# A three-layer graph attention network on one core: the first item's rows turned in the accumulator banks, and a new order of the prologue

## The chip, the core and the metric

The kernel runs on one core of a Trainium2 chip. Its engines work side by side, each through its own list of instructions in order: TensorE (PE, matmuls and their weight loads), VectorE (DVE), ScalarE (ACT), GpSimd (POOL) and SyncE (SP), whose queue issues all DMA transfers here. Engines wait for each other only through semaphores. The metric is the time of one execution on the device in microseconds.

## What is computed

64 graphs of 128 nodes with 256 features each. The input is normalised and cut at zero, three layers of attention over the adjacency and of a two-matrix feed-forward part follow, and the input is added at the end:

```
h = jnp.maximum(_layernorm(x, axis=-1), 0.0)
for l in range(3):
    si = x @ attn_w[l, :d];  sj = x @ attn_w[l, d:]
    scores = si[:, :, None] + sj[:, None, :] + attn_b[l]
    scores = jnp.where(scores >= 0, scores, 0.2 * scores)
    attn = jax.nn.softmax(jnp.where(mask, scores, -jnp.inf), axis=-1)
    agg = jnp.einsum('bij,bjd->bid', attn, x)
    h = layernorm(x + agg, g1[l], beta1[l])
    ff = jax.nn.gelu(h @ W1[l] + b1[l], approximate=False) @ W2[l] + b2[l]
    x = layernorm(h + ff, g2[l], beta2[l])
```

(the loop starts from x = h; the result is the kernel's input plus the last x).

## The kernel before

An **item** is four graphs in one layer: 16 groups of four graphs times three layers, 48 items, in batches of four groups. The work is a pipeline over items. In slot s the feed-forward part of item s runs on TensorE, while the other engines prepare items s + 1 to s + 4. The slots are one written list for each engine, the same for all s. Ahead of the first slot every engine has a **prologue**, written out by hand for items i0 to i3; its order is what the change is about.

One item goes through these steps. Names are the functions of the code.

- `input_moments`, `input_shift` (DVE), `make_rstd` (POOL), `first_x` (ACT): the first normalisation, only in layer 0. `penalty` (DVE) turns the adjacency into a mask.
- `j_dots`, `i_dots` (DVE): the two dot products of every node. The sj values go to DRAM and come back as rows for all partitions (`send_sj`, `load_sj` on SP, tile sj_bc); only item 0 takes them through TensorE (`sj_rows`).
- `masked`, `minus_max` (DVE), `leaky`, `exps` (ACT): scores, row maximum, exponentials in sc.
- The exponentials are turned. Items 0 and 1 (q < BY_PE) do it on TensorE (`e_turn`, into util) and ScalarE copies them out (`et_out`). Later items use `turn_e` (DVE) and DMA (`send_e`, `move_e`).
- `aggregate` (PE) into the banks mix, then `attend`, `moments1`, `norm1` (DVE, with `make_rstd` on POOL between the last two). `h_gamma` and `h_beta` (POOL) make the residual's copy.
- The rows are turned for the matmuls, in two sets of four 128 by 128 blocks. Items 0 and 1 do it on TensorE (`z1_turn`, into util), later ones on VectorE and DMA. ScalarE scales and rounds them (`h_out`, `h_high`, tile ht_hi), VectorE makes what is left over (`h_low`, tile ht_lo).
- The feed-forward part works in eight **chunks** of hidden rows. `ffn1` is six matmuls into one of three banks hbank, ScalarE computes gelu and the rounded copy (`gelu_high`, tile hid_hi), VectorE the low half (`low`, tile hid_lo), `ffn2` is twelve matmuls into the two accumulator banks acc. `ffn1` of a chunk waits until `low` of the chunk three before is done, `ffn2` of a chunk until its own `low` is done.
- `residual`, `moments2`, `shift2` (DVE), `norm2` (ACT), `x_gamma`, `x_beta` (POOL) close the item.

Weights come in 12 halves, four for each layer: `load_weights` (SP), rounded by `round_weights` (ACT), the rest by `split_weights` (DVE). The first eight loads lie in the prologue, and halves 4 to 7 wait for a staging tile that an earlier half leaves.

PSUM has eight banks: three hbank, two acc, two mix and one util. Util is used by all turns on TensorE, and each of them waits until the reader of the one before is done:

```
            def wait_util_read():
                wait(pe, eto_n, read["e"])
                wait(pe, htlo_n, read["z"])
                wait(pe, mask_n, read["s"])
```

So the second set of item 0's rows can't be written before ht_lo of the first set is made, and the first set not before the exponentials of item 1 have been copied out. The acc banks are empty until the first `ffn2`.

Of the kernel before, what the change touches and what calls it, by code (L numbers as in the profile page):

```python
# [33 lines left out]
P = 128  # L34
# [22 lines left out]
def build(nc, x, adj, attn_w, attn_b, W1, b1, W2, b2, g1, beta1, g2, beta2, out):  # L57
# [19 lines left out]
    with ExitStack() as ctx:  # L77
# [232 lines left out]
        def _(sp):  # L310
# [153 lines left out]
            load_xraw(item(2))  # L464
            load_adj(item(2))
            load_weights(4)
            send_sj(i1)
            load_xraw(i3)
            load_sj(i1)
            send_sj(i2)  # L470
            load_weights(5)
            load_adj(i3)
            load_sj(i2)
            load_weights(6)
            send_e(i2)
            send_sj(i3)
            move_e(i2)
            load_sj(i3)
            load_ln2_rows()
            load_attn_rows(False)  # L480
            load_weights(7)
            for s in range(1, ITEMS + 3):
# [10 lines left out]
        def _(pool):  # L493
# [119 lines left out]
            make_rstd("0", i0.g)  # L613
            make_rstd("0", i1.g)
            make_rstd("0", i2.g)
            bias_rows()
            make_rstd("1", i0.q)
            h_gamma(i0, 0)
            h_gamma(i0, 1)
            h_beta(i0, 0)  # L620
            make_rstd("0", i3.g)
            make_rstd("1", i1.q)
            h_beta(i0, 1)
            h_gamma(i1, 0)
            make_rstd("1", i2.q)
            h_gamma(i1, 1)
            h_gamma(i2, 0)
            h_beta(i1, 0)
            for s in range(1, ITEMS + 3):
# [5 lines left out]
        def _(dve):  # L635
# [289 lines left out]
            masked(i0)  # L925
            split_weights(0)
            minus_max(i0)
            j_dots(i1)
            split_weights(1)
            split_weights(2)  # L930
            input_moments(i2)
            i_dots(i1)
            attend(i0, 0)
            input_shift(i2)
            masked(i1)
# [3 lines left out]
            j_dots(i2)  # L939
            penalty(i2)  # L940
            norm1(i0)
            input_moments(i3)
            h_low(i0, 0)
            attend(i1, 0)
            masked(i2)
            h_low(i0, 1)
            attend(i1, 1)
            i_dots(i2)
            moments1(i1)
            split_weights(3)  # L950
            minus_max(i2)
            penalty(i3)
            low(i0, 0)
            input_shift(i3)
            norm1(i1)
            turn_e(i2)
            low(i0, 1)
            split_weights(4)
            j_dots(i3)
            low(i0, 2)  # L960
            low(i0, 3)
            split_weights(5)
            low(i0, 4)
            low(i0, 5)
            h_low(i1, 0)
            i_dots(i3)
            low(i0, 6)
            attend(i2, 0)
            masked(i3)
            attend(i2, 1)  # L970
            h_low(i1, 1)
            moments1(i2)
            minus_max(i3)
            low(i0, 7)
            low(i1, 0)
            norm1(i2)
            residual(i0, 0)
            residual(i0, 1)
            for s in range(1, ITEMS + 3):
# [5 lines left out]
        def _(act):  # L985
# [20 lines left out]
            def h_out(i, m):  # L1006
                if i.q < BY_PE:
                    act.wait_ge(zt_n, KD * i.q + m + 1)
                    if i.q == 0 and m == 0:
                        act.wait_ge(vec_ready, 1)  # L1010
                    act.activation(util[:], util[:], ACT.Identity, bias=beta1c(i.l, m),
                                   scale=g1c(i.l, m)).then_inc(ht_n, 1)
# [81 lines left out]
            first_x(i0)  # L1094
            round_weights(0)
            round_weights(1)
            round_weights(2)
            first_x(i1)
            leaky(i0)
            round_weights(3)  # L1100
            exps(i0)
            et_out(i0)
            first_x(i2)
            leaky(i1)
            exps(i1)
            et_out(i1)
            h_high(i0, 0)
            round_weights(4)
            h_high(i0, 1)
            round_weights(5)  # L1110
            gelu_high(i0, 0)
            leaky(i2)
            exps(i2)
            gelu_high(i0, 1)
            first_x(i3)
            gelu_high(i0, 2)
            gelu_high(i0, 3)
            gelu_high(i0, 4)
            h_high(i1, 0)
            gelu_high(i0, 5)  # L1120
            gelu_high(i0, 6)
            h_high(i1, 1)
            gelu_high(i0, 7)
            leaky(i3)
            gelu_high(i1, 0)
            gelu_high(i1, 1)
            round_weights(6)
            exps(i3)
# [5 lines left out]
        def _(pe):  # L1134
# [114 lines left out]
            e_turn(i1)  # L1249
            z1_turn(i0, 0)  # L1250
            aggregate(i1, 0)
            aggregate(i1, 1)
            z1_turn(i0, 1)
            ffn1(i0, 0)
            ffn1(i0, 1)
            ffn1(i0, 2)
            ffn1(i0, 3)
            ffn2(i0, 0)
            z1_turn(i1, 0)
            ffn2(i0, 1)  # L1260
            ffn1(i0, 4)
            ffn1(i0, 5)
            ffn1(i0, 6)
            ffn2(i0, 2)
            ffn2(i0, 3)
            ffn1(i0, 7)
            aggregate(i2, 0)
            aggregate(i2, 1)
            z1_turn(i1, 1)
            ffn2(i0, 4)  # L1270
            ffn2(i0, 5)
            ffn1(i1, 0)
            ffn1(i1, 1)
            ffn2(i0, 6)
            ffn2(i0, 7)
            ffn1(i1, 2)
# [24 lines left out]
```

## Time and profile before

| | us |
|---|---|
| median of 3 runs (1233.28 to 1233.67) | 1233.32 |
| the profiled execution | 1233.53 |
| its span, first to last instruction | 1231.7 |
| TensorE busy | 1190.9 (97%) |
| VectorE busy | 1058.8 (86%) |
| ScalarE busy | 988.7 (80%) |
| GpSimd busy | 677.0 (55%) |

The page gives busy time for each engine over the whole span. Since the kernel is one pipeline with a start and an end, such a share doesn't say where an engine stood still. For that there are the list of waits (who waited for whom, for how long), the windows (busy time of each engine in a stretch, with TensorE's granted clock, 1.00 for full and 0.50 for half), the timeline (instructions in order) and the chain that ended last.

### The profile page before, as it was taken

How to read it: one execution, taken by the hardware profiler on the slowest of the kernel's cores; microseconds unless marked ns; L12 is line 12 of the kernel's file. 1: busy time of each engine (PE TensorE's matmuls, PEld its weight loads, DVE VectorE, ACT ScalarE, POOL GpSimd, SP SyncE). 2: the span in 40 equal slices, each digit the busy share in tenths (PEclk: the TensorE clock that was granted, in tenths of full speed). 3: DMA queues.
4: the chain of work that ended last, by engine and by line, in shares of the span. 5: the costliest groups of instructions: out<-in, count | busy, mean ns of one | idle time of the engine just before them, and what ended most of it. 6: DMA issues, size and time to landing. Idle time of an engine off the chain costs nothing.

```text
span 1231.7 us, 23195 instructions
## 1 busy us (share of the span) xinstructions
PE 1190.9 (97%) x7325; PEld 1086.1 (88%) x7325; DVE 1058.8 (86%) x3483; ACT 988.7 (80%) x1944; POOL 677.0 (55%) x648
## 2 busy tenths in 40 slices
PE   2799999999999999999999999999999999999997
PEld 1698999999899999999999999999999999999996
DVE  7889888899998888889998888889999888888754
ACT  5777888789888887888888778878888788788853
POOL 2326544556675455546765555455657554645474
PEclk9799999999999999999999999999999999999999
DMA  7243233235432322244344222233454222222322
GB/s 235 62 144 87 78 117 87 73 95 154 147 112 81 102 76 61 85 115 123 116 129 128 87 61 86 88 86 87 126 156 134 83 86 86 69 61 91 116 70 69
DMA packets 142744, 124.73 MB, mean 101 GB/s; under 512 B 16632, under 2 KB 123164, under 8 KB 142620
## 3 DMA queue, kind: packets, MB, share of 16 engines
q1 hardware_dynamic: 142620, 123.23, 33.6%
q8 instruction: 58, 0.95, 0.3%
q14 instruction: 66, 0.54, 0.2%
HBM read 78.53 MB, written 44.66 MB: 100 GB/s over the span
## 4 chain that ended last, share of the span: by engine, by line
PE 92%; DVE 4%; ACT 1%; POOL 1%; issue 1%; DMA 0%; SPq 0%; DVEq 0%; POOLq 0%
PE acc L1164 43%; PE hbank L1149 41%; PE mix L1181 7%; DVE junk L768 0%; DVE xs L836 0%; DVE hid_lo L667 0%; DMA adji<-in_adj_dram 0%; DVE st L843 0%; ACT xs L1061 0%; POOL rstd L511 0%; DVE xs L849 0%; DVE junk L777 0%; DVE sc L804 0%; DVE st L655 0%; POOL hb L538 0%
## 5 line engine op out<-in xcount | busy, mean ns | idle before, releaser
L1164 PE MATMUL acc<-w2hi,hid_hi 128*128 128x256 f32 x1536 | 443.5, 289 | 1.3 <-DVE hid_lo L667 1.3
L1164 PE MATMUL acc<-w2hi,hid_lo 128*128 128x256 f32 x1536 | 434.9, 283 | 0.0
L1164 PE MATMUL acc<-w2lo,hid_hi 128*128 128x256 f32 x1536 | 434.7, 283 | 0.0
L994 ACT ACTIVATE hbank<-hbank,vec 128x512 f32<-128x512 f32 x384 | 254.4, 662 | 139.6 <-PE hbank L1149 133.8
L1149 PE MATMUL hbank<-ht_hi,w1hi 128*128 128x512 f32 x768 | 303.2, 395 | 4.7 <-DVE hid_lo L667 3.7
L1164 PEld LDWEIGHTS acc<-w2hi,hid_hi 128*128 128x128 f32 x1536 | 294.6, 192 | 12.8 <-DVE hid_lo L667 2.4
L1164 PEld LDWEIGHTS acc<-w2lo,hid_hi 128*128 128x128 f32 x1536 | 293.9, 191 | 10.4
L1149 PE MATMUL hbank<-ht_lo,w1hi 128*128 128x512 f32 x768 | 302.4, 394 | 0.0
L1149 PE MATMUL hbank<-ht_hi,w1lo 128*128 128x512 f32 x768 | 299.4, 390 | 0.0
L667 DVE TENSOR_TENSOR hid_lo<-hbank,hid_hi 128x512 fp32r<-128x512 f32 x384 | 258.9, 675 | 41.5 <-ACT hid_hi L1000 41.1
L1164 PEld LDWEIGHTS acc<-w2hi,hid_lo 128*128 128x128 f32 x1536 | 293.8, 191 | 0.0
L1000 ACT CAST hid_hi<-hbank 128x512 fp32r<-128x512 f32 x384 | 225.8, 588 | 12.9 <-PE acc L1164 0.8
L531 POOL TENSOR_TENSOR hb<-xs,ln_rows 128x512 f32<-128x512 f32 x96 | 123.5, 1303 | 151.6 <-DVE xs L681 111.6
L550 POOL TENSOR_TENSOR xs<-xs,ln_rows 128x512 f32<-128x512 f32 x64 | 82.9, 1295 | 179.2 <-DVE dots L777 179.0
L1149 PEld LDWEIGHTS hbank<-ht_hi,w1lo 128*128 128x128 f32 x768 | 144.7, 188 | 32.0
L1149 PEld LDWEIGHTS hbank<-ht_hi,w1hi 128*128 128x128 f32 x768 | 145.5, 189 | 29.4 <-DVE hid_lo L667 4.3
L1149 PEld LDWEIGHTS hbank<-ht_lo,w1hi 128*128 128x128 f32 x768 | 145.6, 190 | 21.0
L509 POOL TENSOR_SCALAR ve<-mv 128x4 f32<-128x4 f32 x111 | 30.4, 274 | 175.8 <-DVE mv L646 175.7
L538 POOL TENSOR_TENSOR hb<-hb,ln_rows 128x512 f32<-128x512 f32 x96 | 124.9, 1301 | 0.0
L511 POOL TENSOR_TENSOR rstd<-ve,halfs 128x4 f32<-128x4 f32 x111 | 118.4, 1067 | 9.3
L836 DVE SCALAR_TENSOR_TENSOR xs<-mix,rden,xs 128x256 f32<-128x256 f32 x192 | 83.7, 478 | 42.4 <-PE mix L1181 41.6
L768 DVE CUSTOM_DVE_ANT_0 junk<-xs,attn_rows 128x256 bf16<-128x256 f32 x192 | 76.6, 455 | 35.5 <-ACT xs L1030 35.1
(91 smaller groups left out, 1777.7 us busy)
## 6 DMA issues: line engine op xcount, KB each, us to landing
z_dram<-tz SPq DMA_DIRECT2D x46, 512.0 KB, 2.6
zt<-z_dram SPq DMA_DIRECT2D x184, 128.0 KB, 3.0
sj_bc<-sj_dram SPq DMA_DIRECT2D x47, 256.0 KB, 3.6
e_dram<-te SPq DMA_DIRECT2D x46, 256.0 KB, 2.0
ET<-e_dram SPq DMA_DIRECT2D x184, 64.0 KB, 2.1
out_dram<-xout SPq DMA_DIRECT2D x32, 256.0 KB, 4.0
xraw<-in_x_dram SPq DMA_DIRECT2D x15, 512.0 KB, 5.1
xres<-in_x_dram SPq DMA_DIRECT2D x15, 512.0 KB, 4.3
```

Source lines behind the costliest of these rows:

```text
L511: pool.tensor_tensor(rstd[n][:], ve[n][:], halfs[:], ALU.pow).then_inc(rstd_n[n], 1)
L531: pool.tensor_tensor(hb[:, i.q % 2, gs], x_of(i)[:, gs], rows_of(ln1_rows[:, 0], i.l), ALU.mult).then_inc(hgam_n, 1)
L538: pool.tensor_tensor(t, t, rows_of(ln1_rows[:, 1], i.l), ALU.add).then_inc(hb_n, 1)
L550: pool.tensor_tensor(t, t, rows_of(ln2_rows[:, 0], i.l), ALU.mult).then_inc(gam_n, 1)
L667: dve.tensor_tensor(hid_lo[:, k % HID], hbank[k % HB][:], hid_hi[:, k % HID].bitcast(F32), ALU.subtract).then_inc(lo_n, 1)
L768: last = dve.tensor_tensor_reduce(junk[:, g], x_of(i)[:, g], attn_rows[:, i.l, 1], 1.0, 0.0, ALU.mult, ALU.add, dots[:, 1, g:g + 1])
L836: dve.scalar_tensor_tensor(out=x_of(i)[:, g], in0=mix_of(i, h)[:, g % HG], scalar=rden[:, g:g + 1], in1=x_of(i)[:, g], op0=ALU.mult, op1=A ...
L994: act.activation(hbank[k % HB][:], hbank[k % HB][:], ACT.Gelu, bias=b1c(i.l, c)).then_inc(gelu_n, 1)
L1000: act.copy(hid_hi[:, k % HID], hbank[k % HB][:]).then_inc(hi_n, 1)
L1149: mm = pe.matmul(hbank[k % HB][:], w[:, i.l, m, at_c], v[:, i.q % 2, m], start=m == 0 and n == 0, stop=m == KD - 1 and n == 2)
L1164: mm = pe.matmul(to, v[:, k % HID, of_g], w[:, i.l, c], start=c == 0 and n == 0 and g % HG == 0, stop=c == C - 1 and n == 2, skip_group_ch ...
L1181: mm = pe.matmul(mix_of(i, h)[:, g % HG], turned, x_of(i)[:, g], start=g % HG == 0, stop=True, skip_group_check=True)
```

## The change

Two things change, both ahead of the first slot.

First, `z1_turn` of item 0 writes its two sets into acc[0] and acc[1] instead of util, without waiting for util's readers; `h_out`, `h_high` and `h_low` of item 0 read them there. Item 1 goes on using util.

```
+        def turned_in(q, m):
+            if q == 0:
+                return acc[m][:].rearrange("p g d -> p (g d)")
+            return util[:]
...
             def z1_turn(i, m):
-                wait_util_read()
+                if i.q > 0:
+                    wait_util_read()
+                t = turned_in(i.q, m)
                 read["z"] += 1
                 for g in range(GG):
                     pe.wait_ge(z1_n, GG * i.q + g + 1)
-                    mm = pe.transpose(util[:, g * P:(g + 1) * P], x_of(i)[:, g, m * P:(m + 1) * P], ident[:])
+                    mm = pe.transpose(t[:, g * P:(g + 1) * P], x_of(i)[:, g, m * P:(m + 1) * P], ident[:])
                 mm.then_inc(zt_n, 1)
...
-                dve.tensor_tensor(ht_lo[:, i.q % 2, m], util[:], ht_hi[:, i.q % 2, m].bitcast(F32),
+                dve.tensor_tensor(ht_lo[:, i.q % 2, m], turned_in(i.q, m), ht_hi[:, i.q % 2, m].bitcast(F32),
...
-                act.copy(ht_hi[:, i.q % 2, m], util[:]).then_inc(hthi_n, 1)
+                act.copy(ht_hi[:, i.q % 2, m], turned_in(i.q, m)).then_inc(hthi_n, 1)
```

Second, the prologue's lists of all five engines are written in another order, with the same calls in each. The slots and the end are as they were. On SP the send of item 1's sj values now goes ahead of weight half 4, item 3's adjacency and weight half 5 go ahead of the send for item 2, and weight half 7 ahead of the load for item 3:

```
             load_xraw(item(2))
             load_adj(item(2))
+            send_sj(i1)
             load_weights(4)
-            send_sj(i1)
             load_xraw(i3)
+            load_adj(i3)
             load_sj(i1)
+            load_weights(5)
             send_sj(i2)
-            load_weights(5)
-            load_adj(i3)
             load_sj(i2)
```

On GpSimd `bias_rows` goes ahead of item 2's `make_rstd`, the `h_gamma` steps of item 1 ahead of the second `h_beta` of item 0.

TensorE, from the turn of item 1's exponentials to the first matmul of `ffn1`. L1206 and L1213 are `z1_turn`, L1181 and L1186 `aggregate` of item 1. Before:

```order
L1214 MATMUL util<-ident,sc 128x128 x4
L1206 MATMUL util<-ident,xs 128x128 x4
L1181 MATMUL mix0<-xs,ET 128x256 x2
L1181 MATMUL mix1<-xs,ET 128x256 x2
L1206 MATMUL util<-ident,xs 128x128 x4
L1149 MATMUL hbank0<-ht_hi,w1hi 128x512
```

and in the changed kernel:

```order
L1221 MATMUL util<-ident,sc 128x128 x4
L1213 MATMUL acc0<-ident,xs 128x128 x4
L1213 MATMUL acc1<-ident,xs 128x128 x4
L1186 MATMUL mix0<-xs,ET 128x256 x2
L1186 MATMUL mix1<-xs,ET 128x256 x2
L1154 MATMUL hbank0<-ht_hi,w1hi 128x512
```

Both sets of item 0 now stand ahead of item 1's aggregation. Further on, the fifth chunk of `ffn1` stands ahead of the first `ffn2`, and item 1's first turn moves from behind the first chunk of `ffn2` to behind its fourth.

VectorE, around the first low halves of hidden rows (tile hid_lo; te is the turn of item 2's exponentials, the TENSOR_SCALAR on xs is `norm1` of item 1, BN_STATS st1 its `moments1`). Before:

```order
L843 BN_STATS st1<-xs 128x6 x4
L644 MEMSET spare 128x1
L646 BN_AGGR mv1<-st1 128x2 x4
L639 TENSOR_TENSOR w2lo<-xres,w2hi 128x1024
L812 ISA below,spare<-msj,dots 128x4
L812 ISA spare 128x1
L788 SCALAR_TENSOR_TENSOR pen<-adji,diag 128x512
L792 TENSOR_SCALAR pen<-pen 128x512
L667 TENSOR_TENSOR hid_lo<-hbank0,hid_hi 128x512
L661 SCALAR_TENSOR_TENSOR nmr0<-mv0,rstd0 128x4
L849 TENSOR_SCALAR xs<-xs,mv1,rstd1 128x256 x4
L820 STREAM_TRANSPOSE te<-sc 128x4x4x32
```

and in the changed kernel:

```order
L672 TENSOR_TENSOR hid_lo<-hbank1,hid_hi 128x512
L644 TENSOR_TENSOR w2lo<-xres,w2hi 128x1024
L817 ISA below,spare<-msj,dots 128x4
L817 ISA spare 128x1
L841 SCALAR_TENSOR_TENSOR xs<-mix1,rden,xs 128x256 x2
L672 TENSOR_TENSOR hid_lo<-hbank2,hid_hi 128x512
L644 TENSOR_TENSOR w1lo<-xout,w1hi 128x1024
L666 SCALAR_TENSOR_TENSOR nmr0<-mv0,rstd0 128x4
L672 TENSOR_TENSOR hid_lo<-hbank0,hid_hi 128x512
L848 BN_STATS st1<-xs 128x6 x4
L649 MEMSET spare 128x1
L651 BN_AGGR mv1<-st1 128x2 x4
```

Four low halves (the first stands a few rows further up) are now ahead of the moments of item 1; before, the first stood behind them.

ScalarE, from the first gelu on (sc,den is `exps` of item 2, the ACTIVATE on sc,dots its `leaky`). Before:

```order
L994 ACT_TABLE_LOAD
L994 ACTIVATE hbank0<-hbank0,vec 128x512
L1000 CAST hid_hi<-hbank0 128x512
L1037 ACTIVATE sc<-sc,dots 128x128 x4
L1042 ACTIVATE negm<-below 128x4
L1047 ACT_TABLE_LOAD
L1047 ACTIVATE sc,den<-sc,negm 128x128 x4
L994 ACT_TABLE_LOAD
L994 ACTIVATE hbank1<-hbank1,vec 128x512
```

and in the changed kernel:

```order
L999 ACTIVATE hbank0<-hbank0,vec 128x512
L1005 CAST hid_hi<-hbank0 128x512
L999 ACTIVATE hbank1<-hbank1,vec 128x512
L1005 CAST hid_hi<-hbank1 128x512
L999 ACTIVATE hbank2<-hbank2,vec 128x512
L1005 CAST hid_hi<-hbank2 128x512
L1042 ACTIVATE sc<-sc,dots 128x128 x4
L999 ACTIVATE hbank0<-hbank0,vec 128x512
L1005 CAST hid_hi<-hbank0 128x512
L1047 ACTIVATE negm<-below 128x4
L1052 ACT_TABLE_LOAD
L1052 ACTIVATE sc,den<-sc,negm 128x128 x4
```

The exponentials of item 2, with a table load on each side, stand behind four gelus instead of one. The roundings of weight halves 4 and 5 move from between the high halves of item 0 to the front and behind item 1's exponentials.

## Rows read from the trace of the kernel before

**Rows 1.** The page, part 1: busy time, share of the span, instructions.

```profile
PE 1190.9 (97%) x7325; PEld 1086.1 (88%) x7325; DVE 1058.8 (86%) x3483; ACT 988.7 (80%) x1944; POOL 677.0 (55%) x648
```

**Rows 2.** TensorE's waits (total, times, longest) to 110 and later; timeline at 94.42.

```profile
PE hbank L1149 <- DVE hid_lo L667: 3.2, 1, 3.2
PE acc L1164 <- DVE hid_lo L667: 1.3, 1, 1.3
...
PE hbank L1149 <- DVE hid_lo L667: 0.5, 1, 0.5
...
94.42 0.38 PE L1164 MATMUL acc<-w2hi,hid_hi 128*128 128x256 f32 x1 [1.25 <-DVE hid_lo L667]
```

**Rows 3.** Windows: length, busy time of each engine, granted clock, DMA share, GB/s.

```profile
28.97:77.03 48.06, 40.02 (x199) 33.92 (x200) 41.90 (x138) 35.94 (x75) 14.45 (x15) 0.82 0.29 88
...
76.99:94.42 17.43, 16.18 (x100) 14.69 (x98) 16.46 (x50) 14.18 (x29) 7.97 (x8) 1.00 0.44 130
```

**Rows 4.** Timeline of VectorE: start, us, instruction, idle before.

```profile
28.97 1.41 DVE L843 BATCH_NORM_STATS2 st<-xs 128x6 f32<-128x256 f32 x4
...
30.71 0.39 DVE L768 CUSTOM_DVE_ANT_0 junk<-xs,attn_rows 128x256 bf16<-128x256 f32 x1
...
32.07 0.68 DVE L788 SCALAR_TENSOR_TENSOR pen<-tz,diag 128x512 bf16<-128x512 int32 x1
...
33.00 2.32 DVE L849 TENSOR_SCALAR xs<-xs,mv,rstd 128x256 f32<-128x256 f32 x4
35.24 1.39 DVE L655 BATCH_NORM_STATS2 st<-xraw 128x6 f32<-128x256 f32 x4
...
41.55 0.69 DVE L855 TENSOR_TENSOR ht_lo<-util,ht_hi 128x512 fp32r<-128x512 f32 x1 [1.02 <-ACT ht_hi L1023]
...
44.56 1.40 DVE L843 BATCH_NORM_STATS2 st<-xs 128x6 f32<-128x256 f32 x4
```

**Rows 5.** Timeline of GpSimd: the root of item 0's variance.

```profile
31.28 1.07 POOL L511 TENSOR_TENSOR rstd<-ve,halfs 128x4 f32<-128x4 f32 x1
```

**Rows 6.** The chain that ended last, pieces on TensorE: start, us, what.

```profile
35.85 3.41 PE mix L1181 x8
39.26 0.87 PE util L1206 x4
...
49.16 2.92 PE hbank L1149 x6
52.08 2.56 PE acc L1164 x12
...
70.16 2.75 PE hbank L1149 x12
72.91 2.89 PE acc L1164 x24
```

**Rows 7.** Timeline of ScalarE at the first gelu.

```profile
42.48 1.28 ACT L994 ACT_TABLE_LOAD   x1
43.78 0.66 ACT L994 ACTIVATE hbank<-hbank,vec 128x512 f32<-128x512 f32 x1
44.47 0.59 ACT L1000 CAST hid_hi<-hbank 128x512 fp32r<-128x512 f32 x1
```

**Rows 8.** Timeline of VectorE: the normalisations of items 1 and 2.

```profile
49.11 3.29 DVE L849 TENSOR_SCALAR xs<-xs,mv,rstd 128x256 f32<-128x256 f32 x4
...
73.51 1.60 DVE L849 TENSOR_SCALAR xs<-xs,mv,rstd 128x256 f32<-128x256 f32 x4
```

**Rows 9.** Windows of half a microsecond; the third number from the end is the clock.

```profile
41.00:41.50 0.50, 0.33 (x1) 0.00 (x0) 0.00 (x0) 0.50 (x2) 0.00 (x0) 0.88 0.00 0
47.50:48.00 0.50, 0.00 (x0) 0.00 (x0) 0.50 (x3) 0.38 (x2) 0.42 (x2) 0.95 0.00 0
```

**Rows 10.** Tiles sj_bc and xout (weights) up to 90: transfers, issue to landing.

```profile
DMA to landing us min/median/max: 3.6/3.7/5.5
...
DMA to landing us min/median/max: 3.6/5.0/7.1
```

More of the change, by code:

```diff
@@ L465, in _ @@
             load_adj(item(2))
+            send_sj(i1)
             load_weights(4)
-            send_sj(i1)
             load_xraw(i3)
+            load_adj(i3)
             load_sj(i1)
+            load_weights(5)
             send_sj(i2)
-            load_weights(5)
-            load_adj(i3)
             load_sj(i2)
+            send_e(i2)
             load_weights(6)
-            send_e(i2)
+            move_e(i2)
             send_sj(i3)
-            move_e(i2)
+            load_weights(7)
             load_sj(i3)
@@ L943, in _ @@
             h_low(i0, 0)
+            penalty(i2)
+            h_low(i0, 1)
             attend(i1, 0)
+            i_dots(i2)
+            low(i0, 0)
             masked(i2)
[L946 to L949, printed above, removed]
+            low(i0, 1)
             split_weights(3)
             minus_max(i2)
-            penalty(i3)
[L953 to L967, printed above, removed]
+            attend(i1, 1)
+            low(i0, 2)
+            split_weights(4)
+            input_shift(i3)
+            low(i0, 3)
+            moments1(i1)
+            turn_e(i2)
+            split_weights(5)
+            norm1(i1)
+            low(i0, 4)
+            j_dots(i3)
+            low(i0, 5)
+            i_dots(i3)
+            h_low(i1, 0)
+            low(i0, 6)
+            penalty(i3)
             attend(i2, 0)
+            low(i0, 7)
+            attend(i2, 1)
             masked(i3)
-            attend(i2, 1)
             h_low(i1, 1)
             moments1(i2)
+            residual(i0, 0)
             minus_max(i3)
-            low(i0, 7)
+            residual(i0, 1)
             low(i1, 0)
             norm1(i2)
-            residual(i0, 0)
-            residual(i0, 1)
             for s in range(1, ITEMS + 3):
@@ L1010, in h_out @@
                         act.wait_ge(vec_ready, 1)
-                    act.activation(util[:], util[:], ACT.Identity, bias=beta1c(i.l, m),
-                                   scale=g1c(i.l, m)).then_inc(ht_n, 1)
+                    t = turned_in(i.q, m)
+                    act.activation(t, t, ACT.Identity, bias=beta1c(i.l, m), scale=g1c(i.l, m)).then_inc(ht_n, 1)
                 else:
@@ L1095, in _ @@
             round_weights(0)
+            first_x(i1)
             round_weights(1)
-            round_weights(2)
-            first_x(i1)
             leaky(i0)
-            round_weights(3)
             exps(i0)
             et_out(i0)
+            round_weights(2)
+            round_weights(3)
             first_x(i2)
             leaky(i1)
+            round_weights(4)
             exps(i1)
+            round_weights(5)
             et_out(i1)
             h_high(i0, 0)
-            round_weights(4)
             h_high(i0, 1)
-            round_weights(5)
             gelu_high(i0, 0)
+            gelu_high(i0, 1)
+            gelu_high(i0, 2)
             leaky(i2)
+            gelu_high(i0, 3)
             exps(i2)
-            gelu_high(i0, 1)
+            gelu_high(i0, 4)
             first_x(i3)
-            gelu_high(i0, 2)
-            gelu_high(i0, 3)
-            gelu_high(i0, 4)
+            gelu_high(i0, 5)
             h_high(i1, 0)
-            gelu_high(i0, 5)
             gelu_high(i0, 6)
+            gelu_high(i0, 7)
+            round_weights(6)
             h_high(i1, 1)
-            gelu_high(i0, 7)
             leaky(i3)
@@ L1257, in _ @@
             ffn1(i0, 3)
+            ffn1(i0, 4)
             ffn2(i0, 0)
-            z1_turn(i1, 0)
             ffn2(i0, 1)
-            ffn1(i0, 4)
+            ffn2(i0, 2)
             ffn1(i0, 5)
             ffn1(i0, 6)
-            ffn2(i0, 2)
             ffn2(i0, 3)
+            z1_turn(i1, 0)
             ffn1(i0, 7)
+            ffn2(i0, 4)
+            ffn2(i0, 5)
             aggregate(i2, 0)
@@ L1269, in _ @@
             z1_turn(i1, 1)
-            ffn2(i0, 4)
-            ffn2(i0, 5)
+            ffn2(i0, 6)
+            ffn2(i0, 7)
             ffn1(i1, 0)
             ffn1(i1, 1)
-            ffn2(i0, 6)
-            ffn2(i0, 7)
             ffn1(i1, 2)
```

24 lines of the change are left out of this document (11 added, 13 removed).

## The prediction

> **What bounds the kernel now.** Start with the page: TensorE is busy for 1190.9 us of a span of 1231.7 [rows 1]. The list of who waits for whom shows how little of its idle time lies late: after 110 us it waits once, for 0.5 us, and the two last waits before that, 3.2 and 1.3 us, both for VectorE's low halves, lie in the first 95 us [rows 2]. Behind 95 us the program is TensorE's own work, which the change doesn't touch. What the change can move is the moment from which TensorE runs through, 94.42, when the 1.3 us wait ends [rows 2]. The windows say who sets it: from 28.97 to 77.03 TensorE has 40.02 us of work, part of it at half clock, and VectorE 41.90 in 48.06; from 76.99 to 94.42 TensorE has 16.18 in 17.43, with full clock [rows 3]. So at the last wait TensorE is ahead and VectorE, which works through a fixed order, is late. The question is how much sooner VectorE gets through its prologue, and then whether TensorE can follow.
>
> **Fixed marks.** All positions are microseconds of the profiled execution; i0 to i3 are items 0 to 3. VectorE's list ahead of the moments of i0 (28.97) holds the same operations in both kernels, and so does its list from there to the transpose of i2 that starts at 77.03; only the order differs. Up to 28.97 I find no gain and no loss: weight halves 1 and 2 are split behind i2's moments now, but ScalarE's exponentials of i0, which release the first aggregation, begin as before, and the aggregation is the later input.
>
> **Up to the first matmul of ffn1.** The moments of i0 run from 28.97 to 30.71, the dots of i2 to 32.07. Before, the penalty of i2 stood next (0.93) and the normalisation started at 33.00 [rows 4]. Now it stands there at once, but GpSimd's reciprocal root ends at 31.28 + 1.07 = 32.35 [rows 5], so VectorE waits 0.3, and the four instructions (2.24) end at 34.65 instead of 35.24: 0.6 sooner. TensorE turns the rows of i0 into the two accumulator banks, eight transposes in a row. Four took 0.87 [rows 6], so the first bank is complete at 35.3 and the second at 36.1; before, the second set shared util, stood behind the aggregation of i1, and was complete at 40.1. The price: the aggregation of i1 (3.41 for eight matmuls at half clock [rows 6]) starts at 36.1 instead of 35.85 and ends at 39.5. ScalarE and VectorE work on both banks under it, so the two low halves are done at 37.4 and 38.9. The first matmul of ffn1 starts at 39.5, and nothing interrupts the chunk.
>
> **VectorE's first real wait.** From 28.97 its work ahead of the first low half of hidden rows is moments twice 1.74, dots of i2 1.36, normalisation 2.24, penalty 0.93, a low half 0.6, the other low half with the attention update and the second dots 3.01 (41.55 to 44.56) and a reciprocal 0.2 [rows 4]: 11.8. With 0.3 for the root and 0.35 for the first high half it is free at 41.4. Six matmuls of ffn1 from 39.5, the first at 0.43 and the rest at 0.229 (2.75 for twelve [rows 6]), end at 41.4 to 41.7. Gelu and rounding start 0.69 apart and the rounding takes 0.59 [rows 7]: low half 0 starts at 42.7, after a wait of 1.3. The table load of 1.28 [rows 7] lies in ScalarE's empty time before 39.5 and costs nothing; without that cover it would cost its 1.28.
>
> **VectorE from there.** Its work in the whole stretch is 41.90 [rows 3]. Two items change length. The normalisation of i1 took 3.29 while GpSimd worked beside it on two steps; that of i2 took 1.60 and that of i0 2.32 [rows 4, 8]. In the new order GpSimd's beta step of i0 stands behind, so I take 2.3 for i1 (1.0 less) and 2.0 for i2, since a gamma step falls beside it (0.4 more). From 42.7 there remain 41.9 - 11.8 - 0.6 = 29.5, so the transpose of i2 starts at 72.2 if nothing is late. What each step needs, worked out on ScalarE with 1.18 per gelu and rounding: three of them end at 45.3, the leaky step of i2 at 46.5, gelu 3 at 47.7, then 0.2, a table load of 1.28 and exponentials of 1.6, done at 50.8; VectorE wants them at 51.5. A second table load and gelu 4 end at 53.3 (wanted at 56.0), the first inputs of i3 at 55.3 (56.6), gelu 5 at 56.5 (58.0). The last matmul of ffn2 for i0 ends at 66.1 (68.2), gelu 0 of i1 at 68.9 (69.6). All are covered, the tightest by 0.7. The copies of the score rows are less sure (rival 1), for which I add 0.2. Then 77.03 becomes 72.4: **4.6 us sooner**. The same from the waits: before, 48.06 - 41.90 = 6.2 us [rows 3]; now 0.3 + 0.35 + 1.3 + 0.2 = 2.1, and 0.6 less work: 4.7.
>
> **TensorE's side.** Chunks 0 to 2 of ffn1 run from 39.5, chunks 3 and 4 need low halves 0 and 1, done at 43.3 and 45.2: no gap, so the 3.2 us wait goes, and with it the half clock behind it, at which twelve matmuls of ffn2 took 2.56 against 1.45 [rows 6]. From 39.5: 11 chunks of ffn1 at 1.37, 8 of ffn2 at 1.45, 2.3 for the aggregation and the turns, 0.6 for the slow first matmuls and 1.3 of waiting near 56 for the normalisation of i1 and low half 4 give 70.4 for the prologue's last matmul, instead of 76.99: 6.6 sooner. VectorE grants only 4.6, so 2 us come back as new waits in the first slot, on low halves 1, 2 and 5 of i1 (0.8, 0.6 and about 1.6, against the one of 1.3). The lesser gain counts. In that slot nothing is reordered, and what VectorE waits for there, GpSimd's root and ScalarE's second normalisation, hangs on VectorE's own moments and moves with it. I take off 0.1 for small starts: **4.5**. The profiled execution took 1233.53 for its span of 1231.7; less 4.5 is 1229.0, and the median of the runs lies 0.2 below that execution: 1228.8.
>
> **The clock.** The granted clock is back at full by 41.5 (0.88 in the half microsecond before), after work without a break since 35.4, and falls just before 48 (0.95) [rows 9], two microseconds after TensorE went idle at 46.0, 3.2 ahead of 49.16 [rows 2, 6]. In the new order work is unbroken from 34.8, so the rise could come 0.6 sooner or at the same 41.1; I take the middle. If it came at 38, VectorE's 1.3 us wait would vanish. The 1.3 us wait before 94.42 did not cost the clock [rows 2, 3]; a wait of 1.6 lies between the cases. The Trainium skill, page "TensorE: Matmul & The Clock Gate", section "HAM oscillation — how this bites in real kernels", tells of a kernel whose TensorE fell back to the low clock in every wait between bursts. [...]
>
> **Rivals.** (1) Late row copies. VectorE's masks of i1 and i3 need the broadcast copy of sj, which landed 3.6 to 5.5 us after its issue [rows 10]. For i1 it is wanted at 26.8; the send now goes ahead of weight half 4, which helps, but i3's adjacency is queued ahead of the copy, which hurts. For i3 weight half 7 is queued just ahead; sent at 58.0 and two microseconds on its way, the copy lands at 63.6 to 65.5 and is wanted at 64.7. Each late microsecond is one of VectorE's. Late by 1.0 and 0.8, the gain is 2.9 and the time 1230.4. (2) The clock falls in the wait before low half 5, which may last 1.5 to 2.0. Half clock for some 5.5 us of work costs 2.7: gain 1.8, time 1231.5. (3) Early clock: gain 5.8, time 1227.5. (4) Slower. ScalarE's rounding of weight half 5 now stands ahead of the copy of i1's exponentials, and holds ScalarE and the aggregation of i1. Its load is issued behind the split of half 1, near 24; it is wanted at 32.1, with slack to 34. From there each microsecond costs one, so from a landing at 41 the kernel is slower by over 0.2%: 1237 with one at 42. Against it: the prologue's weight loads landed in 3.6 to 7.1 [rows 10], and it needs 17. (5) The waits only change place: something else in the first slot, such as GpSimd's order, keeps 94.42 within 1 us: 1232.5. Against it: GpSimd has little to do there.
>
> **How the numbers follow.** Forecast 0.52; late copies 0.14; clock 0.12; early clock 0.10; nothing reaches the end 0.08; slower 0.04. The range takes in the early clock, the forecast, the copies and the drop: 1227.0 to 1231.8. A measurement of this kernel tells about 0.2%, 2.5 us, from no change, so faster means below 1230.8: forecast, early clock, most of the late copies and a little of the rest, 0.77; same 0.19; slower 0.04.
>
> **What would show it.** Right: eight transposes into acc at 34 to 36, no wait of VectorE over 0.5 us between 43 and 72, its transpose of i2 at 72 to 73, TensorE at full clock from about 41, and waits on low halves of some 3 us in the first slot. Wrong: half clock after 85, a wait on sj_bc, a wait on weight half 5 near 32; and the whole reasoning, if 4.6 us at the transpose are not 4.6 us at the end.

## The result and the profile after

The changed kernel takes 1235.64 us (median of 20 runs, 1234.85 to 1238.47), the kernel before 1233.48 beside it (20 runs, 1232.87 to 1235.1). The ratio is 1.0018, 95% interval 1.0012 to 1.0024. By the bound of the prediction, 0.2%, that is no change; the interval says that it is a loss, of 2.2 us. The forecast was a gain of 4.5, with 1231.8 as the slowest time of its range. It was wrong.

The profiled execution took 1236.37, its span is 1234.6. The page, part 1, beside [rows 1]:

```profile
PE 1190.2 (96%) x7325; PEld 1083.7 (88%) x7325; DVE 1064.1 (86%) x3483; ACT 988.3 (80%) x1944; POOL 676.9 (55%) x648
```

TensorE has the same work. VectorE is busy for 5.3 us more with the same 3483 instructions. That number points at the cause: not an operation was added, so some of them took longer.

The waits to 110 us, of TensorE (beside [rows 2]) and of VectorE: who waited, for whom, total, times, longest.

```profile
PE acc L1169 <- DVE hid_lo L672: 3.3, 2, 1.8
...
DVE sc L809 <- DMA sj_bc<-sj_dram: 2.6, 2, 1.4
...
PE hbank L1154 <- DVE ht_lo L860: 1.7, 1, 1.7
...
PE hbank L1154 <- DVE hid_lo L672: 1.3, 2, 1.0
...
DVE nmr L666 <- POOL rstd L516: 0.9, 1, 0.9
```

The two waits for row copies, that of i1 and that of i3, in VectorE's timeline:

```profile
30.09 0.38 DVE L809 CUSTOM_DVE_ANT_0 sc<-pen,sj_bc 128x128 f32<-128x128 bf16 x1 [1.29 <-DMA sj_bc<-sj_dram]
...
71.47 0.38 DVE L809 CUSTOM_DVE_ANT_0 sc<-pen,sj_bc 128x128 f32<-128x128 bf16 x1 [1.35 <-DMA sj_bc<-sj_dram]
```

The windows, beside [rows 3] (length, busy time of PE, PEld, DVE, ACT and POOL, granted clock, DMA share, GB/s). The second begins and ends at the same two instructions of VectorE as the first of [rows 3], the moments of i0 and the transpose of i2:

```profile
28.97:77.03 48.06, 38.04 (x199) 31.39 (x199) 44.80 (x143) 34.96 (x72) 14.53 (x15) 0.89 0.26 82
32.17:79.26 47.09, 40.27 (x211) 33.34 (x212) 44.92 (x137) 35.48 (x73) 15.93 (x16) 0.89 0.24 74
```

The moments of i0 start at 32.17 instead of 28.97, so 3.2 us are lost ahead of the place where the prediction's working began. In the stretch behind it VectorE has 44.92 us of work in 47.09. Before it had 41.90 in 48.06. The waits shrank as forecast, from 6.2 to 2.2, but 3.0 us of work came in their place. In sum the transpose starts at 79.26, 2.2 later than before, and TensorE restarts 2.1 later than at 94.42. The chain that ended last shows this restart, on VectorE's low half:

```profile
95.00 0.88 DVE xs L841 x2
95.88 0.61 DVE hid_lo L672
96.48 0.04 issue
96.53 1.70 PE acc L1169 x12
```

Where the work got longer, VectorE's timeline tells (start, us, instruction, idle before). L773 is one of the four dots of an item over its rows (`j_dots`), L797 the second step of `penalty`:

```profile
18.24 0.42 DVE L773 CUSTOM_DVE_ANT_0 junk<-xs,attn_rows 128x256 bf16<-128x256 f32 x1
...
18.58 2.02 DVE L773 CUSTOM_DVE_ANT_0 junk<-xs,attn_rows 128x256 bf16<-128x256 f32 x1
...
41.21 1.26 DVE L797 TENSOR_SCALAR pen<-pen 128x512 bf16<-128x512 bf16 x1
...
59.06 1.11 DVE L773 CUSTOM_DVE_ANT_0 junk<-xs,attn_rows 128x256 bf16<-128x256 f32 x1
...
60.10 1.51 DVE L773 CUSTOM_DVE_ANT_0 junk<-xs,attn_rows 128x256 bf16<-128x256 f32 x1
...
61.55 1.49 DVE L773 CUSTOM_DVE_ANT_0 junk<-xs,attn_rows 128x256 bf16<-128x256 f32 x1
...
62.97 0.41 DVE L773 CUSTOM_DVE_ANT_0 junk<-xs,attn_rows 128x256 bf16<-128x256 f32 x1
```

And GpSimd's timeline of the same execution (L521 is `bias_rows`, L536 `h_gamma`, L543 `h_beta`):

```profile
18.42 1.90 POOL L521 TENSOR_TENSOR ln_rows<-ln_rows,hb 128x768 f32<-128x768 f32 x1 [2.87 <-DMA ln_rows<-in_L_gnn_beta_dram]
24.52 1.11 POOL L514 TENSOR_SCALAR ve<-mv 128x4 f32<-128x4 f32 x1 [4.20 <-DVE mv L651]
...
41.06 1.26 POOL L536 TENSOR_TENSOR hb<-xs,ln_rows 128x512 f32<-128x512 f32 x1
...
58.61 1.28 POOL L536 TENSOR_TENSOR hb<-xs,ln_rows 128x512 f32<-128x512 f32 x1 [0.23 <-DVE xs L854]
59.85 2.90 POOL L543 TENSOR_TENSOR hb<-hb,ln_rows 128x512 f32<-128x512 f32 x2
```

Read the two together. `bias_rows` ends at 18.42 + 1.90 = 20.32; the dot that began at 18.58 ends at 20.60, 0.3 after that. The penalty ends at 42.47, just behind the gamma step (42.32). The three slow dots of i3 end 0.3 after one GpSimd step each (59.89, and 61.3 and 62.75, half and whole of the 2.90). None of this stands in the list of waits, since the instruction had started: it counts as busy. It goes the other way too: GpSimd's small step at 24.52 takes 1.11, and ends when VectorE's split of a weight half does (24.35 + 1.19).

**Theory.** A GpSimd operation and certain VectorE operations exclude each other, and the later one stands until the earlier is done. The new order puts GpSimd's long steps beside such operations in three places, for 1.6, 1.0 and 2.9 us, and VectorE's splits beside GpSimd's root of i2, for which VectorE then waits 0.9. A second cause is rival (1), 2.6 us of waiting for row copies. **Rivals:** the list of GpSimd only moves the stall (the step has to run somewhere); the banks, not the order, do the harm; the early microseconds are lost in the transfers alone.

### The profile page after: what moved, and what is told of

It reads as the page before. It is cut to its first block, busy times and chain, and to the rows that moved or that the text cites. A ratio compares the mean times of both kernels' runs of the same rounds, so it can differ in the third digit from the quotient of the medians.

```text
span 1234.6 us, 23192 instructions
## 1 busy us (share of the span) xinstructions
PE 1190.2 (96%) x7325; PEld 1083.7 (88%) x7325; DVE 1064.1 (86%) x3483; ACT 988.3 (80%) x1944; POOL 676.9 (55%) x648
## 4 chain that ended last, share of the span: by engine, by line
PE 89%; DVE 7%; DMA 2%; issue 1%; ACT 1%; POOL 0%; SPq 0%; DVEq 0%
PE acc L1169 42%; PE hbank L1154 40%; PE mix L1186 7%; DVE junk L773 1%; DMA sj_bc<-sj_dram 1%; DVE hid_lo L672 1%; DVE xs L854 1%; DVE sc L809 0%; DVE xs L841 0%; DMA tz<-in_adj_dram 0%; DVE st L848 0%; DVE junk L782 0%; DMA sj_dram<-dots 0%; POOL rstd L516 0%; DVE ht_lo L860 0%
## 5 line engine op out<-in xcount | busy, mean ns | idle before, releaser
L536 POOL TENSOR_TENSOR hb<-xs,ln_rows 128x512 f32<-128x512 f32 x96 | 123.4, 1302 | 149.9 <-DVE xs L686 108.6
L543 POOL TENSOR_TENSOR hb<-hb,ln_rows 128x512 f32<-128x512 f32 x96 | 125.0, 1302 | 0.0
L773 DVE CUSTOM_DVE_ANT_0 junk<-xs,attn_rows 128x256 bf16<-128x256 f32 x192 | 81.0, 477 | 35.4 <-ACT xs L1035 35.3
```

The lines of the kernel that those rows point to most:

```text
L536: pool.tensor_tensor(hb[:, i.q % 2, gs], x_of(i)[:, gs], rows_of(ln1_rows[:, 0], i.l), ALU.mult).then_inc(hgam_n, 1)
L543: pool.tensor_tensor(t, t, rows_of(ln1_rows[:, 1], i.l), ALU.add).then_inc(hb_n, 1)
L773: last = dve.tensor_tensor_reduce(junk[:, g], x_of(i)[:, g], attn_rows[:, i.l, 1], 1.0, 0.0, ALU.mult, ALU.add, dots[:, 1, g:g + 1])
```

## The experiments

All runs beside the kernel before on the same chip, where it took 1233.4 to 1233.6 us. "tr." is the start of VectorE's transpose of i2 in the profiled execution.

| kernel | us (runs) | ratio to before, 95% | profiled | tr. |
|---|---|---|---|---|
| before | 1233.48 (20) | | 1233.53 | 77.03 |
| after | 1235.64 (20) | 1.0012 to 1.0024 | 1236.37 | 79.26 |
| e1_bias_back | 1233.85 (11) | 0.9994 to 1.0012 | 1233.24 | 77.69 |
| k7_before_bias_moved | 1235.13 (11) | 1.0002 to 1.0020 | 1235.30 | 77.95 |
| e2_pool_back | 1234.73 (11) | 1.0001 to 1.0019 | 1234.72 | 78.91 |
| k8_steps_off_dots | 1232.86 (11) | 0.9987 to 1.0005 | 1232.86 | 75.65 |
| e3_copies | 1233.37 (11) | 0.9990 to 1.0008 | 1233.06 | 77.22 |
| e4_acc_alone | 1232.86 (11) | 0.9986 to 1.0004 | 1233.82 | 77.19 |
| k5_bias_and_copies | 1233.47 (11) | 0.9985 to 1.0002 | 1231.98 | 76.28 |
| k6_pool_timed_and_copies | 1229.19 (5) | 0.9951 to 0.9976 | 1228.56 | 72.21 |
| m3_k6_again | 1229.36 (6) | 0.9955 to 0.9978 | 1230.67 | 73.90 |
| m1_good_order_util | 1231.32 (11) | 0.9974 to 0.9991 | 1231.05 | 74.72 |
| m2_i1_copy_first | 1228.35 (5) | 0.9941 to 0.9968 | 1228.84 | 72.26 |

The profiled time less the last column is 1155.6 to 1157.4 in all of them: what VectorE's transpose of i2 gains or loses, the end gains or loses, within a microsecond. Two profiles of one kernel (k6 and m3) differ by 1.7 at that place. So a trace tells what happened in it, and the medians tell what an edit is worth.

**bias_rows, out of the changed kernel and into the old one.** In e1:

```
             make_rstd("0", i1.g)
-            bias_rows()
             make_rstd("0", i2.g)
+            bias_rows()
```

> The changed kernel with one swap undone: GpSimd's bias_rows stands behind the reciprocal root of item 2 again. Theory 1 (GpSimd's tensor_tensor beside VectorE's instructions that read two tiles on chip stalls VectorE): the dot that took 2.02 us in the changed kernel takes 0.42 again, item 2's root takes 1.1 and not 1.9, VectorE reaches its masks of item 1 some 2 us sooner, and since the copy of sj hangs on these dots too, the end comes about 1.6 us sooner: 1234.0. Theory 2 (only the copies of sj are late, because of the loads queued around them): the dots keep near 2 us wherever they stand, the end moves by less than 0.4. Theory 3 (VectorE's new order as such is slower, whatever runs beside it): no change, 1235.6.

k7 is the reverse: the kernel before with only this swap made.

> The kernel before with one swap of the change and nothing else: GpSimd's bias_rows ahead of item 2's root. Theory 1: a dot of item 1 near 18.5 takes 2.0 us and not 0.42, and the short shift of item 2 that took 0.40 takes 0.16; the rest is 1.3 later, 1234.8. Theory 3 (VectorE's new order is what costs): no change, 1233.5.

e1 gained 1.8, k7 lost 1.6. VectorE's timeline of e1: the dots of i1 are all short, and it is now the small shift of i2 that stands behind `bias_rows`.

```profile
18.73 0.42 DVE L773 CUSTOM_DVE_ANT_0 junk<-xs,attn_rows 128x256 bf16<-128x256 f32 x1
...
25.56 1.77 DVE L666 SCALAR_TENSOR_TENSOR nmr<-mv,rstd 128x4 f32<-128x4 f32 x1
```

GpSimd in e1:

```profile
25.27 2.03 POOL L521 TENSOR_TENSOR ln_rows<-ln_rows,hb 128x768 f32<-128x768 f32 x1
```

VectorE in k7, in the old order:

```profile
18.42 2.02 DVE L768 CUSTOM_DVE_ANT_0 junk<-xs,attn_rows 128x256 bf16<-128x256 f32 x1
```

One edit puts the stall on the dot and its reverse takes it off again, in either kernel. In e1 the operation still costs VectorE 1.6, but it no longer pushes back the send of i1's rows, so no wait for their copy follows. In the kernel before, the shift met only the end of `bias_rows` (0.40 us).

**GpSimd's list.** e2 gives the changed kernel the whole GpSimd list of before (`bias_rows` too). From the first beta step on:

```
+            make_rstd("0", i3.g)
             make_rstd("1", i1.q)
+            h_beta(i0, 1)
             h_gamma(i1, 0)
-            h_gamma(i1, 1)
-            h_beta(i0, 1)
-            h_beta(i1, 0)
             make_rstd("1", i2.q)
+            h_gamma(i1, 1)
             h_gamma(i2, 0)
+            h_beta(i1, 0)
```

> The changed kernel with the whole prologue list of GpSimd as before the change, so that no beta step of items 0 and 1 stands beside the dots of item 3. Theory 1: besides the 1.6 us of the bias step, the three dots of 1.11, 1.51 and 1.49 us go back to 0.42 (2.9 us less); the beta step of item 0 now lies beside the normalisation of item 1 and costs up to 1.0 there. Sum 3.5 sooner, less what the copy for item 3 takes back if it is not sooner too: 1232.1, between 1231 and 1233.5. Theory 2: under 0.5 us of gain, since the wait for the copy of item 3 absorbs the rest. Theory 3: 1235.6.

This missed, by 2.6. The dots of i3 were short again (0.41), but VectorE's list of waits from 30 to 110 has one that is in neither kernel:

```profile
DVE xs L686 <- POOL hb L536: 2.9, 1, 2.9
```

The residual of i0 writes into the tile that i1's rows leave, free only when `h_gamma(i1, 1)` has read them, and that step now stood behind the root of i2 and started at 73.16; VectorE wanted the tile at 71.8. The normalisation of i1, now beside the second beta step of i0, took 3.30 instead of 2.32, as expected. So the gain went into a wait and a new stall: the old list fits the old order only. The penalty of i2, which no gamma step meets in e2, took 0.29 again. e2 couldn't separate the theory from the first rival, so k8 leaves the order of VectorE alone and holds the steps back by waits on its progress:

```
             h_beta(i0, 0)
+            pool.wait_ge(lo_n, 4)
+            h_beta(i0, 1)
             make_rstd("1", i1.q)
             h_gamma(i1, 0)
+            pool.wait_ge(dots_n, 4)
             h_gamma(i1, 1)
-            h_beta(i0, 1)
-            h_beta(i1, 0)
             make_rstd("1", i2.q)
             h_gamma(i2, 0)
+            h_beta(i1, 0)
```

> The changed kernel with GpSimd's late part timed alone: the second beta of item 0 ahead of item 1's root and waiting for the fourth low half, the second gamma of item 1 waiting for the dots of item 3, the first beta of item 1 last. Bias step, copies and everything else as changed. Theory 1: the dots of item 3 take 0.42 each, 2.9 us less; the copy for item 3 is sent as much sooner, so 2.7 reach the end: 1232.9. Theory 2: the copy's queue doesn't move, the wait for it grows, and under 1 us reaches the end: 1234.8.

2.8 us better than after, on the number that was expected. VectorE and, below it, GpSimd in k8: the second gamma step of i1 starts only when all dots of i3 are done.

```profile
59.41 0.41 DVE L775 CUSTOM_DVE_ANT_0 junk<-xs,attn_rows 128x256 bf16<-128x256 f32 x1
```

```profile
57.00 1.40 POOL L536 TENSOR_TENSOR hb<-xs,ln_rows 128x512 f32<-128x512 f32 x1 [1.30 <-DVE xs L856]
62.83 1.30 POOL L536 TENSOR_TENSOR hb<-xs,ln_rows 128x512 f32<-128x512 f32 x1 [4.43 <-DVE dots L784]
```

So the first rival falls for these steps: there are places where they cost next to nothing, beside operations that read PSUM (0.1 us on the penalty of i3, 0.80 instead of 0.68, where the gamma step's end meets it).

**The row copies.** e3 is the changed kernel with SyncE's list as before: weight half 4 ahead of i1's send, i3's adjacency and half 5 behind i1's copy, half 7 behind i3's copy.

> The changed kernel with three places of SyncE's list undone: weight half 4 ahead of the send of item 1, item 3's adjacency behind the load of item 1's copy, weight half 7 behind the load of item 3's copy. GpSimd's list stays as changed. Theory 2: VectorE's waits for the copies, 1.3 and 1.35 us, fall to 0.3 or less each, and the end comes 2.0 to 2.6 us sooner: 1233.3. Theory 1: the copy for item 1 still hangs on the stalled dots; waits shorter by what the queue made of them, 1 to 1.5 us in all: 1234.4. Theory 3: 1235.6.

2.3 us better than after, with no wait for a copy left and the dots as slow as in after. i1's copy landed in 4.2 instead of 5.9, i3's in 5.0 instead of 6.5. So the wait for i3's copy has a cause of its own. That for i1's copy goes with either edit, e1's or e3's: the copy is late because its send waits for the stalled dot and because of the loads around it.

**The banks alone** in the kernel before, with all lists as they were:

> The kernel before with the accumulator banks for item 0's turns and nothing of the new order. All theories: the second set still stands behind item 1's aggregation, and the reader of the first set was done 1.1 us before that, so nothing becomes free: 1233.4 within 0.5. If the banks themselves cost something (a conflict with the first ffn2 or a slower read of acc), it is slower here too, by 1 us or more.

Nothing that can be measured: 0.6 us less, with no change inside the interval. The banks aren't what costs time. The second set still stands behind the aggregation of i1 in e4, and TensorE's timeline shows what else keeps the gain small: the wait of 3.2 us of [rows 2] is still in it, since the first low half stands behind the moments of i1 in the old order.

```profile
49.36 0.51 PE L1154 MATMUL hbank<-ht_hi,w1hi 128*128 128x512 f32 x1 [3.16 <-DVE hid_lo L672]
```

**Together.** k5 joins e1 and e3:

> The changed kernel with bias_rows back behind item 2's root and the three places of SyncE's list for the copies undone, together. The first alone gave 1.8 us at the end, the second 2.2. If the shared read path and the late copies are two separate losses: 4.0 together, 1231.6. If the copy for item 1 had hidden the stall of the bias step, so that either cure brings the same gain: 1233.0.

The trace is near the sum (76.28, where 79.26 - 1.6 - 2.0 would be 75.7), but the profiled execution was the quickest of the eleven. The median, 1233.47, is 2.2 better than after, where the two edits alone gave 1.8 and 2.3: it misses the sum that was expected and lies nearer to the rival. The traces show one reason. Both edits remove the same wait, the 1.29 us for i1's copy, so the moments of i0 start 1.7 sooner than in after with e1, 1.1 with e3 and only 1.9 with both. Only the 1.35 for i3's copy is e3's alone. Whether that is all that is missing stays open. k6 joins k8 and e3, and holds `bias_rows` back until item 1's dots are done, so that it runs beside the moments of i2. It also puts the first root of i3 behind the first beta step of i0, as before, which moves that beta step and the gamma step ahead of it off the penalty:

```
             make_rstd("0", i1.g)
+            pool.wait_ge(dots_n, 2)
             bias_rows()
```

> The changed kernel with SyncE's three places undone and GpSimd's prologue timed so that its tensor_tensor steps lie beside VectorE's instructions that read one tile on chip: bias_rows waits for the dots of item 1 and runs beside item 2's moments, both gamma steps of item 0 go ahead of item 3's root, the second beta of item 0 waits for the fourth low half and runs beside item 1's moments, the second gamma of item 1 waits for the dots of item 3, the first beta of item 1 goes last. Theory 1 with theory 2: 2.5 us from the bias step, 2.2 from the copies, 2.9 from the dots of item 3, 1.0 from the penalty of item 2, less about 0.5 for new starts: 1227.5, between 1226.5 and 1229.5. If stalls beside GpSimd are only moved about: 1231 or more, as with the copies and the bias step.

1229.19 us, faster than both kernels, and 1.7 above the number that was expected. One wait is left: VectorE now comes to i1's copy sooner and waits 1.27 for it. A second set (m3_k6_again) gave 1229.36, with 2.16 of that wait in its trace:

> The order with the timed GpSimd steps and the row copies as before a second time, unchanged, as the reference for the two others on the same chip: 1229.2 (1228.6 to 1229.8), transpose of item 2 at 72.2. The rival, that 1229.19 was a lucky set of five runs, gives 1231 or more, which is what the trace of its profiled execution would then have missed.

VectorE and GpSimd in k6, where `bias_rows` now runs:

```profile
20.85 1.40 DVE L663 BATCH_NORM_STATS2 st<-zt 128x6 f32<-128x256 f32 x4
```

```profile
21.01 1.81 POOL L521 TENSOR_TENSOR ln_rows<-ln_rows,hb 128x768 f32<-128x768 f32 x1 [5.63 <-DVE dots L785]
```

The four moments take the 1.40 that they take anywhere [rows 4], although GpSimd works beside them from 21.01 on. And VectorE's windows from the moments of i0 to the transpose of i2 in k6:

```profile
29.77:72.21 42.44, 39.02 (x211) 33.37 (x212) 41.26 (x137) 35.35 (x72) 14.76 (x16) 1.00 0.24 82
```

The same 137 instructions as in after's second window take 41.26 us instead of 44.92. That is 3.7 less, where the penalty and the dots of i3 had been 3.9 longer in after. With the waits down to 1.2 the stretch is 4.7 shorter. From after to k6 the medians say 6.4; e1, e3 and k8, each alone, gave 1.8, 2.3 and 2.8, together 6.9.

**What the banks are worth in the good order.** m1 is k6 with util for both sets of item 0, with `z1_turn` waiting for util's readers again and the second set behind the aggregation:

```
-            if q == 0:
-                return acc[m][:].rearrange("p g d -> p (g d)")
             return util[:]
...
             z1_turn(i0, 0)
-            z1_turn(i0, 1)
             aggregate(i1, 0)
             aggregate(i1, 1)
+            z1_turn(i0, 1)
```

> The order that left GpSimd's long steps away from VectorE's dots and sent the row copies as before (1229.19 us, VectorE's transpose of item 2 at 72.21), with the accumulator banks taken out of it: both sets of item 0 are turned in util again, with util's waits, and the second set stands behind item 1's aggregation. Theory: there VectorE has no other work left to hide the turn. The second set is complete at 40.2 instead of 36.8, so item 0's second low half starts at 41.6 instead of 39.04, 2.5 us later, of which the wait of 0.4 for the first gelu gives some back: VectorE's transpose of item 2 at 74.3, time 1231.3 (1230.8 to 1231.8). Rival: the banks are worth as little as in the order of before, where they alone gave 0.0005 of the time: then 1229.2 to 1229.8 and a transpose at 72.2 to 72.8.

1231.32, against 1229.36 for m3 on the same chip: 2.0 us, where e4 gave 0.6 in the old order. The two are not the same edit: m1 also gives up the early place of the second set, which the banks make possible and which e4 never had. So 2.0 is what banks and place are worth together. VectorE's waits in m1:

```profile
DVE ht_lo L861 <- ACT ht_hi L1029: 2.6, 2, 2.3
```

m2 is k6 with the send of i1 ahead of weight half 4 on SyncE, and the copy right behind it:

```
+            send_sj(i1)
+            load_sj(i1)
             load_weights(4)
-            send_sj(i1)
             load_xraw(i3)
-            load_sj(i1)
             load_adj(i3)
```

> The same order with the accumulator banks, and on SyncE the copy of item 1's score rows right behind its send, ahead of weight half 4 and item 3's input. Theory: the 1.27 us that VectorE waits for this copy at 27.69 goes, the transpose of item 2 comes at 71.0 to 71.3, time 1228.0 (1227.6 to 1228.6). Weight half 4 is then issued about 5 us later, near 23; its rounding stands at 30.2, later than the 7.1 that the slowest load of the prologue took. Rival: something else, the first aggregation or ScalarE's first high half, holds the stretch behind 29, and the wait only moves there: 1229.2.

1228.35, 1.0 less than m3 and the lowest median of all, though with five and six runs the two intervals overlap, and the transpose was expected at 71.0 to 71.3 and came at 72.26. The wait for the copy is gone (1.3 in k6, 2.2 in m3). Part of it came back, as VectorE's waits in m2 show; in all, the same line is 1.3 in k6 and 0.9 in m3:

```profile
DVE hid_lo L675 <- ACT hid_hi L1008: 2.1, 3, 1.2
```

The 1.2 lies at 42.62, ahead of low half 0, where k6 has 0.38 and m3 nothing. `ffn1` of its chunk began 0.8 sooner than in k6, but its first three matmuls took 1.61 us (38.80 to 40.41) and not 0.88 (39.63 to 40.51). The granted clock of m2 is 0.50 until 40, the low level of 1.2 GHz, and 1.00 only from 40.5: what came next was TensorE's clock.

## Why the prediction was wrong

**The frame held.** VectorE's transpose of i2 sets the end: 2.2 later there, 2.2 later in the medians, and the same in thirteen profiles within a microsecond. That 4.6 us at the transpose are 4.6 at the end was named as the point on which all rests; it stands.

**"Up to 28.97 I find no gain and no loss" was the step that failed.** It was 3.2. The prediction looked there at ScalarE's exponentials and at TensorE's aggregation, and not at GpSimd, though the diff says in one line that `bias_rows` moves. Of the 3.2, 1.6 are on a dot, 0.9 are waiting for the root of i2 (which GpSimd does with 1.11 and 1.89 us, beside two splits, instead of 0.37 and 1.13) and 1.3 waiting for i1's copy; VectorE no longer loses the 0.84 us that it lost there before (0.60 for mix and 0.24 on the shift), and 0.2 are spread over small differences.

**The work of the stretch was taken as 41.3 (41.9 less 0.6) and was 44.9.** With the 3.2 ahead of it, these 3.6 are the whole miss at the transpose, 79.26 instead of 72.4; the waits, 2.2 where 2.1 were forecast, were right in sum. The prediction did size one item by GpSimd, the normalisation of i1: 2.3 expected, 2.32 measured. So it had the effect in its hands, in the row with 3.29 us [rows 8], and treated it as a property of that operation. The steps that left the normalisation went beside the dots of i3, 2.9 us, and the penalty, 1.0. The normalisation of i2 took 2.35, where 2.0 was expected. k6 shows the work with GpSimd's long steps out of the way: 41.26, which is what the prediction had.

**Low half 0** started at 45.60 instead of 42.7, and without the wait of 1.3: 3.2 late from the start, 1.0 by the penalty, less the wait. TensorE's first matmul of ffn1 started at 42.11, not 39.5, right behind the aggregation of i1 as forecast, and late with all the rest. From low half 0 to the transpose it took 33.7 instead of 29.5: the dots 2.9, i3's copy 1.35, the normalisation of i2 0.35, less some 0.4 elsewhere.

**Two sums** of the prediction don't come out as they are written. From 39.5 one matmul at 0.43 and five at 0.229 end at 41.1, not at 41.4 to 41.7; the measured chunk took 2.0 us from its first matmul (42.11) to the gelu (44.12), as the forecast had it and not its terms. And waits of 3.0 in the first slot against the one of 1.3 bring back 1.7, not 2. The first is worth 0.3 of VectorE's wait for low half 0, the second nothing at the end.

**Right** were: the eight transposes one behind the other (at 36.05 to 39.1 and not at 34 to 36, with 0.80 of waiting for the rows among them) and ScalarE's two sets one behind the other (38.49 and 39.75, where before there were 4.3 us between them); no wait of VectorE between 43 and 70; no lost microsecond for the table load, which lay in ScalarE's empty time; no wait on weight half 5 (rival 4). In the first slot TensorE waits 1.0 and 1.6 for low halves, where three waits of 3.0 in all were forecast. Ahead of it, it waits 1.75 (at 64.05, behind the slow dots), where 1.3 near 56 was forecast, and 1.65 for item 1's rows at 73.43, which was not.

**Rival (1)**, late copies, came true and was too small: 1.29 and 1.35 against 1.0 and 0.8. With the loads moved, a copy of 256 KB landed 1.5 to 1.7 later than in e3. These are single traces: with the same SyncE list as e3's, i1's copy took 4.2 there, 4.6 in k6 and 5.6 in m3. That the order of the loads costs time is shown by e3's median, not by the landings. **Rival (2)**, the clock drop, did not. TensorE stood still from 94.98 to 96.53, and the window keeps full clock with no matmul in it at all (after, number of PE's instructions in brackets, clock third from the end):

```profile
95.00:96.00 1.00, 0.00 (x0) 0.00 (x0) 1.00 (x3) 0.97 (x2) 0.92 (x2) 1.00 0.71 43
```

The wait of 1.75 didn't cost it either: the granted clock from 64 to 65 is 1.00 too. The prediction named the Trainium skill, page "TensorE: Matmul & The Clock Gate", section "HAM oscillation — how this bites in real kernels", where TensorE fell back to the low clock in every wait between bursts. The waits that the page draws there are longer, some 3 to 5 us, so it speaks neither for nor against a drop in waits of 1.6; the 3.2 us of the kernel before, behind which the clock was at half [rows 6], is of that length. **Rival (3)**, the early clock, did not come either: it is 0.50 up to 42.0 and 0.93 in the half microsecond behind. **Rival (5)**, the gain lost in the first slot, did not come true as it was written: from the transpose to TensorE's restart it is 17.3 us, where it was 17.4. But what stands against it, "GpSimd has little to do there", is the thought that failed in the prologue: little to do, and yet each step of it can shut out VectorE.

**The forecast for the good order.** With the exclusion and the late copy of i3 taken out, the change gives 1229.2 to 1229.4, where 1228.8 was forecast. That it comes so near is in part luck: in k6 the moments of i0 start 0.8 later than forecast, with the wait for i1's copy still there, and the waits behind them are 1.2 instead of 2.1. The mechanism was right for the banks with the earlier turn (2.0 us in that order) and for the work of the stretch. What failed was to leave GpSimd's list out but for one item, and to size SyncE's too small.

## What to carry to other kernels

When an order is changed, lay GpSimd's list beside VectorE's and look what runs at the same time as each long GpSimd step; put those steps beside moments or operations that read PSUM, if need be by a wait on VectorE's progress. If an engine's busy time grows with the same instructions, look for rows of one group that are longer than the rest, since such a stall stands in no list of waits. And an edit that frees a bank or a buffer may show nothing (0.6 us) until the order uses it and what is late next is out of its way (2.0 us).

## What the runs showed of the hardware

**VectorE and GpSimd exclude each other by operation, whole instruction by whole instruction.** So engines do wait for each other without a semaphore, other than the introduction says. A dot with two SBUF inputs took 2.02 instead of 0.42 beside `bias_rows`, the shift of 4 columns (two SBUF inputs) 1.77 instead of 0.16, the bf16 TENSOR_SCALAR of 512 columns (one input) 1.26 instead of 0.29. The moments (one SBUF input) kept their 1.40, and the low half at 58.46 in after, which reads PSUM, its 0.68 under the gamma step from 58.61; so did the low half at 42.39, which began when the beta step of 42.28 was already running. The Trainium skill, page "SBUF — State Buffer", section "Who interferes with whom", states this rule: a VectorE operation in a mode that uses both ports, or one with two SBUF inputs against a GpSimd operation that reads SBUF, excludes the GpSimd operation, and whoever comes second waits for the whole of the other. The rows above agree with it. I had not weighed it in the prediction, where it speaks against this change.

**The granted clock can be recorded wrongly at the start of a trace.** k6's window above says 1.00, and m3, the same kernel, has 0.50 from 32 to 40. The matmuls show no difference: four transposes took 1.54 in both (at 32.02 and at 33.92). So k6's gain is not a matter of the clock there, and a stretch before the first recorded change has to be judged by the duration of its matmuls.
